# Query and key norms in a merged attention stage: one wide square on ScalarE, sums by head on VectorE, rotated halves added before the norm on GpSimd

## The reference

```python
q = (x @ wq).reshape(B, L, 16, 128); k = (x @ wk).reshape(B, L, 4, 128)
q = rms_norm(q, q_norm_w); k = rms_norm(k, k_norm_w)      # x * rsqrt(mean(x*x) + eps) * w, by head
k_ctx = rms_norm((h_ctx_kv @ wk_ctx).reshape(B, T, 4, 128), k_norm_w)
q = q * cos + rotate_half(q) * sin
k = k * cos + rotate_half(k) * sin                        # k_ctx is not rotated
probs = softmax(q @ concat(k_ctx, k).T / sqrt(128) + mask)
out = (probs @ concat(v_ctx, v)) @ wo
```

## Time and profile before

| | us |
|---|---|
| median of 3 runs | 2677.8 (2677.27 to 2686.52) |
| profiled execution, its own time | 2674.28 |
| its span, first to last instruction | 2672.4 |
| busy: PE / DVE / ACT / POOL | 2308.8 / 1410.1 / 1123.0 / 654.3 |

### The profile page before, as it was taken

The page is one execution under the profiler, slowest core; times in us unless marked ns, Lnnn a source line. Parts: engine busy times, 40 slices in busy tenths (PEclk is TensorE's granted clock), DMA queues, the critical chain, the costliest instruction groups (busy, mean ns, idle before and its releaser), DMA issues. The chain is left out here.

```text
span 2672.4 us, 37871 instructions
## 1 busy us (share of the span) xinstructions
PE 2308.8 (86%) x10712; PEld 1446.3 (54%) x10760; DVE 1410.1 (53%) x3456; ACT 1123.0 (42%) x3406; POOL 654.3 (24%) x894
## 2 busy tenths in 40 slices
PE   6959999999968858885899888988989477869999
PEld 3446767666645534442555555555556244436775
DVE  7951111111145547774567677667667557764233
ACT  2022222222135525553555555655555167763332
POOL 5612222222113320001333333333333100002222
PEclk9959999999989989998999999999999689989999
DMA  6100000000030000000000000000000000022342
GB/s 250 53 7 7 7 6 6 6 6 6 2 140 1 0 3 1 0 0 24 1 1 1 1 0 0 0 0 0 0 0 0 2 5 4 4 97 101 103 126 63
DMA packets 40680, 68.91 MB, mean 26 GB/s; under 512 B 6800, under 2 KB 34448, under 8 KB 39312
## 3 DMA queue, kind: packets, MB, share of 16 engines
q1 hardware_dynamic: 37520, 59.44, 6.5%
q0 software_dynamic: 3072, 8.39, 1.0%
HBM read 51.30 MB, written 16.52 MB: 25 GB/s over the span
## 5 line engine op out<-in xcount | busy, mean ns | idle before, releaser
L820 DVE TENSOR_TENSOR moe_hid<-moe_act_g,moe_pU 128x384 f32<-128x384 f32 x128 | 70.9, 554 | 443.4 <-ACT moe_act_g L792 443.4
L792 ACT ACTIVATE moe_act_g<-moe_pG 128x384 f32<-128x384 f32 x128 | 62.7, 490 | 424.5 <-PE moe_pU L747 424.5
L726 POOL TENSOR_TENSOR moe_hidw<-moe_hid,moe_data_w_all 128x384 f32<-128x384 f32 x128 | 105.7, 826 | 426.7 <-DVE moe_hid L820 419.9
L979 PE MATMUL l2x_pQ<-big,l2x_xT 128*128 128x512 f32 x320 | 161.5, 629 | 39.8 <-POOL l2x_cT L2227 32.8
L2080 ACT ACTIVATE l2x_prob<-l2x_pS,l2x_nb,l2x_rms_q 128x256 f32<-128x256 f32 x256 | 142.5, 565 | 120.0 <-DVE l2x_nb L2306 120.0
L747 PE MATMUL moe_pG<-big,moe_xT 128*128 128x384 f32 x512 | 187.5, 489 | 4.1 <-POOL moe_xT L714 4.1
L768 PE MATMUL moe_pO<-big,moe_hT 128*128 128x256 f32 x768 | 186.8, 379 | 0.0
L747 PE MATMUL moe_pU<-big,moe_xT 128*128 128x384 f32 x512 | 186.3, 486 | 0.0
L2061 ACT ACTIVATE l2x_square<-l2x_pQ 128x128 bf16<-128x128 f32 x384 | 101.4, 292 | 102.2 <-PE l2x_pQ L979 102.2
L768 PEld LDWEIGHTS moe_pO<-big,moe_hT 128*128 128x128 f32 x768 | 136.0, 190 | 13.2
L747 PEld LDWEIGHTS moe_pU<-big,moe_xT 128*128 128x128 f32 x512 | 97.6, 191 | 68.3 <-issue 0.9
(11 more groups left out here) (453 smaller groups left out, 5248.7 us busy)
## 6 DMA issues: line engine op xcount, KB each, us to landing
route_x<-l3f_zero SPq DMA_DIRECT2D x1, 4992.0 KB, 16.3
l3f_xg<-route_x SPq DMA_DIRECT2D x39, 128.0 KB, 2.2
route_y<-l3f_y SPq DMA_DIRECT2D x39, 128.0 KB, 1.7
big<-in_f_gu SPq DMA_DIRECT2D x1, 4096.0 KB, 12.5
big<-in_e_gate SPq DMA_DIRECT2D x1, 3072.0 KB, 10.4
big<-in_e_up SPq DMA_DIRECT2D x1, 3072.0 KB, 17.3
big<-in_e_down SPq DMA_DIRECT2D x1, 3072.0 KB, 24.2
moe_lanes<-in_l2f_lanes SPq DMA_DIRECT2D x16, 192.0 KB, 2.8
```

Source lines behind the costliest of these rows:

```text
L726: pool.tensor_tensor(hidw[c % 2][:].rearrange("p (e i) -> p e i", e=n), hid[c % 2][:].rearrange("p (e i) -> p e i", e=n), bc(w, chunk // n ...
L979: last = pe.matmul(out, lhsT=xT[:, k, :], rhs=w[:, k, cols], start=(k == 0), stop=(k == KC - 1))
```

## The change

ACT squares the whole 128x512 projection in one activation without accumulation, into a single float32 tile `square` (before: two bfloat16 tiles, whose values nothing read). DVE, behind the products of each unit, reduces this tile by head into `ssq` and raises a new semaphore `sum_done`. POOL's `unit` first adds the halves and then does the two small steps of the norm. `key_norm` now always waits for the norm, and `maxima` gets a wait for the norm of its slot's unit. ACT's next square waits for the sums of the unit before.

```diff
-        square = [ph.sb(f"square{i}", [P, 4, P], BF16) for i in range(2)]
+        square = ph.sb("square", [P, 4, P])
...
-                after(act, S["rms_steps"], 2 * (6 * b + u) - 3)
-                for h in range(4):
-                    ins = act.activation(square[u % 2][:, h, :], pQ[:, h * P:(h + 1) * P], ACT.Square,
-                                         accum_out=ssq[u % 2][:, h:h + 1])
-                ins.then_inc(S["sq_done"], 1)
+                after(act, S["sum_done"], 6 * b + u)
+                act.activation(square[:].rearrange("p h d -> p (h d)"), pQ[:], ACT.Square
+                               ).then_inc(S["sq_done"], 1)
...
-                pool.wait_ge(S["sq_done"], U + 1)
-                pool.tensor_tensor(r[:], ssq[u % 2][:], eps128[:], ALU.add).then_inc(S["rms_steps"], 1)
-                pool.wait_ge(S["rms_steps"], 2 * U + 1)
-                pool.tensor_tensor(r[:], r[:], G["minus_half"][:, 0:4], ALU.pow).then_inc(S["rms_steps"], 1)
                 if u != 1:
                     pool.wait_ge(S["mul_done"], U + 1)
                     pool.tensor_tensor(rows[u % 2][:], part[u % 2][0][:], part[u % 2][1][:],
                                        ALU.add).then_inc(S["add_done"], 1)
+                pool.wait_ge(S["sum_done"], U + 1)
+                pool.tensor_tensor(r[:], ssq[u % 2][:], eps128[:], ALU.add).then_inc(S["rms_steps"], 1)
+                pool.wait_ge(S["rms_steps"], 2 * U + 1)
+                pool.tensor_tensor(r[:], r[:], G["minus_half"][:, 0:4], ALU.pow).then_inc(S["rms_steps"], 1)
...
+            def sums_of(b, u):
+                after(dve, S["rms_steps"], 2 * (6 * b + u) - 3)
+                dve.tensor_reduce(ssq[u % 2][:], square[:], AX.X, ALU.add).then_inc(S["sum_done"], 1)
...
                     dve.tensor_tensor(part[1][0][:], q, wide(wrow[:, 1, :]), ALU.mult).then_inc(S["mul_done"], 1)
+                    sums_of(b, u)
                     return
...
                 dve.tensor_tensor(r[:, :, H:P], q[:, :, 0:H], wide(s[:, H:P]), ALU.mult).then_inc(S["mul_done"], 1)
+                sums_of(b, u)
...
             def key_norm(b, p, u):
+                dve.wait_ge(S["rms_steps"], 2 * (6 * b + u) + 2)
...
             def maxima(b, g):
                 N = 4 * b + g
+                dve.wait_ge(S["rms_steps"], 2 * (6 * b + g + 2) + 2)
```

More of the change, by code:

```diff
@@ L1779, in phase_l2 @@
         eps128 = ph.sb("eps128", [P, 4])
-        names = ("const_in", "tables", "cT_ready", "proj_ps", "sq_done", "mul_done", "rms_steps", "add_done",
+        names = ("const_in", "tables", "cT_ready", "proj_ps", "sq_done", "mul_done", "sum_done", "rms_steps", "add_done",
                  "krows_ready", "turned", "turn_read", "v_ps", "v_read", "sc_ps", "max_steps", "nb_ready", "exp_done",
@@ L2290, in key_norm @@
                 else:
-                    dve.wait_ge(S["rms_steps"], 2 * (6 * b + u) + 2)
                     dve.wait_ge(S["mul_done"], 6 * b + u + 1)
```

## The result

The changed kernel takes 2688.9 us in the median of 20 runs (2683.3 to 2697.2), the kernel before 2680.2 in its 20 (2674.0 to 2686.7): ratio 1.0032, interval 1.0021 to 1.0042, + 8.7 us. Forecast were + 4, with a chance of 80% that the change stays within 0.5% either way. The profiled execution took 2685.09 us, with a span of 2683.0 and a mean clock of 0.946, against 2672.4 and 0.949. "A fall" is a stretch in which the granted clock is at its lower level, 1.2 GHz.

What follows compares the result with a forecast made beforehand. PE was taken as the bound, through its own work and pauses. Batches + 0.6, ends of the stage - 2.0 and clock + 4.7 made + 3.3, say + 4 us: a median of 2682 us, range 2668 to 2698.

Steps and rivals of the forecast that it cites:

- the four pauses: PE's waits in each batch that the change touches, A, B, D and E, together 4.78 us before the change.
- The pieces: New instructions: ACT's one 128x512 square out of PSUM at 0.60 us, DVE's sums by head at 0.69.
- D: PE's pause at the end of slot 1, waiting for POOL's copy `cT`: to grow by 0.84, 2.31 to 3.15 us.
- the term 1.38: POOL's time from epsilon to add, now in line ahead of `f_product` and the `cT` copy: 1.38 us added to D.
- E: PE's pause in slot 2, waiting for ACT's copy `probT`: to shrink by 0.50, from 0.98 to 0.48 us.
- The wait of `key_norm` that was costed at nothing: Key scaling after E now waits for the power step; keys were to come at the same time, no cost.
- A + B: PE's slot 3 pauses, A (0.29) for DVE's unit 2 products, B (1.20) for `probT`: together 1.49 to about 1.2 us.
- + 0.04 a batch in all: Sum per batch: E - 0.50, A and B - 0.30, D + 0.84; times 15, + 0.6 us.
- The clock, ten falls at 1.1, + 4.7: TensorE's clock falls after 10 of 15 D pauses at 1.1 us each, against six at 1.05 before: + 4.7 us.
- The sums don't stand still under POOL's add: Rival: DVE's sums out of SBUF held until POOL's add ends, 3.5 us a batch, about 2730 us; chance 5%.
- The waits for `probT` didn't vanish: Rival: E, A and B all vanish, - 1.63 a batch, about 2656 us; 6% together with a D that doesn't grow.
- The clock at every pause and for longer: Rival: the clock falls at all 15 D pauses, 2687 us, or 2704 if each lasts twice as long; chance 8%.

Runs made afterwards that it cites:

- the moved kernel: Changed kernel with 60 small DVE writes ahead of the stage, outside the loop, so its loop body stands elsewhere: 2707.11 us, ratio 0.999 to the kernel before.
- ctx_early kernels: POOL's `cT` copy put at slot 1's start: in the kernel before 2636.33 us (0.984), changed 2631.44 (0.9817), changed with 60 DVE writes ahead 2622.85 (0.9791).
- 24, 40 and 60 writes: Changed kernel with that many small DVE writes ahead of the stage: 2675.04 and 2679.99 us (single executions, beside 2675.78 before); 60: 2707.11, ratio 0.999.
- 12 writes: Changed kernel with 12 small DVE writes ahead of the stage, outside the loop: 2695.24 us in one execution, beside 2678.16 for the kernel before.

## Why the prediction was right

The change of + 8.7 lies 4.7 us above the forecast of + 4, the time of 2688.9 inside the range of 2668 to 2698, and the four pauses changed as they were forecast to. That the sum came so near is in part luck. The step that was missed is the size of DVE's loop body. The prediction counted the time of each added instruction and none for its place in the program; the slot-0 pause of 5 x 1.42 = 7.1 us stands in none of its terms, bounds or rivals. Growing the body alone and moving the loop alone show it from both sides. Without it the forecast would have lain above the measurement: the moved kernel comes out at 0.999, - 2 us, which can't be told from no change.

- *The pieces* (square 0.60, sums 0.69): 0.605 and 0.676. Right.
- *D from 2.31 to 3.15*: 3.03, + 0.72 for + 0.84. The mechanism is right and shown by itself; the term 1.38 was 0.12 too large, since part of it was a wait for `mul_done` that the new order doesn't have. POOL in the changed kernel, 1.26 from epsilon to `f_product`:

```profile
1585.62 0.20 POOL L2198 TENSOR_TENSOR l2x_rms_q<-l2x_ssq,l2x_eps 128x4 f32<-128x4 f32 x1
1585.90 1.01 POOL L2200 TENSOR_TENSOR l2x_rms_q<-l2x_rms_q,minus_half 128x4 f32<-128x4 f32 x1
1586.88 1.26 POOL L2204 TENSOR_TENSOR small<-small 128x512 f32<-128x512 f32 x1
1588.09 0.40 POOL L2225 COPY l2x_cT<-ctxT 128x256 f32 x1
```

- *E from 0.98 to 0.48*: 0.38, - 0.60 for - 0.50. The wait of `key_norm` that was costed at nothing is there, 0.62 us of DVE, and PE's wait ahead of the turning of the keys is 0.23 in both traces.
- *A + B from 1.49 to 1.2*: 1.23, all of it B. Right.
- *+ 0.04 a batch in all*: the four pauses make - 0.14 by their rows (4.78 to 4.64), the windows - 0.29. The other 0.15 is PE's own busy time (46.16 to 46.01), and nothing here settles why. In the ctx_early kernels it is likewise 0.15 (45.92 to 45.77).
- *The clock, ten falls at 1.1, + 4.7*: nine at some 1.36, + 5.7 over the eleven batches. The size is right; the reason given, that D of 3.15 must bring more falls than one of 2.31, isn't borne out. Three executions with the loop moved have the same D of 3.03 and 4, 3 and 0 falls (24, 40 and 60 writes), fewer than before's six at 2.31; the two with the slot-0 pause (changed, and 12 writes) have nine each. Yet the pause by itself, beside a D of 2.31, left the six. The rule of the Trainium skill (TensorE: Matmul & The Clock Gate, section HAM oscillation — how this bites in real kernels) is a fall in each pass. It holds here for a D of 3.57 from the second pause on, nearly for one of 3.62 (eleven of thirteen), and not for one of 3.03. What decides between 2.31 and 3.03 stays open: one execution of each kernel is too little, as the falls may differ from one execution to the next (the trace with none is of the quickest of its kernel's eleven).
- *Rivals.* The sums don't stand still under POOL's add: 0.676 in the mean of 96, and `nb` is held no more. DVE and POOL behind the square of the keys, in the changed kernel:

```profile
1592.52 0.68 DVE L2272 TENSOR_REDUCE l2x_ssq<-l2x_square 128x4 f32<-128x512 f32 x1
1593.12 0.68 DVE L2308 TENSOR_REDUCE l2x_negmax<-l2x_pS 128x2 f32<-128x512 f32 x1
```
```profile
1592.69 1.27 POOL L2195 TENSOR_TENSOR l2x_rows<-l2x_part 128x512 f32<-128x512 f32 x1 [4.20 <-DVE l2x_part L2287]
```

  The add begins while the sums run, both go on side by side for 0.5 us, and the sums take 0.68 all the same. The waits for `probT` didn't vanish. The clock at every pause and for longer isn't in the changed kernel, but D of 3.57 has it, so the changed kernel stands half a microsecond a batch from a loss of 1.3%.

The luck is in terms that partly cancelled: 7.1 us missed, and batches 0.33 quicker than forecast, 5 us over fifteen.

## What to carry to other kernels

Count an engine's instructions in a hardware loop, waits too, as well as their time (whether empty branch targets count isn't shown): where instruction packets rise and an engine stands with "issue" behind a turn, move the loop or shorten it before anything else. Where PE waits for one engine's copy at the end of a queue, put that copy ahead of the work that the change makes longer; here one moved line was worth 1.6%, five times the whole effect of the change. Half of an edit can be worse than none (+ 1.3% and + 1.0%) though both together cost 0.3%, so price the halves on the same pause.

## What the hardware showed unexpectedly

- DVE stood 2.4 to 2.5 us at each turn of a loop whose body had grown from 233 to 268 instructions, with 24 more instruction packets in the execution; PE lost 1.42 of them. The same body 24 instructions further on had no such wait.
- Of the thirteen full pauses of 3.57 us, every one from the second on was followed by the lower clock, from the third on for some 5.6 us; of those of 3.62 us, all but two; of 3.03 us, between none and nine of thirteen, in five executions of kernels that differ in little but the place of a loop.
- A float32 reduction with both ends in SBUF ran its 0.68 us beside POOL's add, under which DVE's products of two SBUF tiles had stood still; the two overlapped for 0.5 us.
